# Who sums the routed rows of tiles 4 to 7 before the second attention: DVE in its prologue, or GpSimd ahead of its first affine

## The reference

```
x = x + tanh(g_xattn[0]) * L0_xattn(layernorm(x), ctx)   # 16 heads of 128
x = x + tanh(g_ffn[0])   * L0_ffn(layernorm(x))          # 64 experts, top 8 of them, and a shared MLP
x = x + tanh(g_xattn[1]) * L1_xattn(layernorm(x), ctx)   # 16 heads of 16, 48 + 16 keys
x = x + tanh(g_ffn[1])   * L1_ffn(layernorm(x))          # 8 experts, top 2, and a shared one
```

## Time and profile before

| what | us |
|---|---|
| median of 3 runs (1355.36 to 1357.71) | 1356.01 |
| profiled execution: its span | 1354.8 |
| PE busy | 1046.2 (77%) |
| DVE busy | 765.6 (57%) |
| ACT busy | 424.9 (31%) |
| POOL busy | 307.7 (23%) |

### The profile page before, as it was taken

How to read it: one execution, slowest core, us unless ns; L and a number is a source line. 1 busy time by engine, 2 the same in 40 slices (tenths; PEclk the granted TensorE clock), 3 DMA queues, 4 the chain that set the end, 5 groups by cost and what they waited for, 6 DMA issues and landing times.

```text
span 1354.8 us, 16681 instructions
## 1 busy us (share of the span) xinstructions
PE 1046.2 (77%) x5397; PEld 863.6 (64%) x5397; DVE 765.6 (57%) x1687; ACT 424.9 (31%) x781; POOL 307.7 (23%) x271
## 2 busy tenths in 40 slices
PE   3989989989885700578772377877879999999997
PEld 2867867868663500467661246464757989899896
DVE  6367567585658889323226897786865324242221
ACT  3554445374533300112120032323252232322321
POOL 0413304223000000577771182630200000000000
PEclk8999989999986755788786565768676989899899
DMA  7008600000000140477765640100000000000001
GB/s 264 1 0 288 211 1 0 0 0 1 1 0 20 39 129 1 142 213 223 213 196 185 245 157 32 64 0 0 0 0 1 1 1 0 0 0 0 0 0 62
DMA packets 63667, 91.24 MB, mean 67 GB/s; under 512 B 5901, under 2 KB 56327, under 8 KB 60807
## 3 DMA queue, kind: packets, MB, share of 16 engines
q1 hardware_dynamic: 56116, 71.42, 16.3%
q0 software_dynamic: 6144, 18.88, 4.5%
q10 hardware_dynamic: 1363, 0.37, 0.1%
HBM read 60.74 MB, written 29.89 MB: 67 GB/s over the span
## 4 chain that ended last, share of the span: by engine, by line
PE 55%; DVE 20%; issue 10%; ACT 5%; POOL 4%; DMA 4%; ACTq 1%; DVEq 0%; POOLq 0%; SPq 0%
PE bank L1993 12%; PE bank L2012 7%; PE bank L1651 4%; PE bank L1696 4%; DMA xg<-table,src_now 3%; PE bank L1921 3%; PE bank L1681 2%; PE bank L1879 2%; PE bank L2004 2%; DVE y_sum L1170 2%; PE bank L1798 2%; PE bank L1938 2%; PE bank L1811 2%; POOL q_lo L481 2%; DVE cand L946 1%
## 5 line engine op out<-in xcount | busy, mean ns | idle before, releaser
L1993 PE MATMUL bank<-gu_hi,xnT_split 128*128 128x352 f32 x640 | 159.5, 329 | 0.0
L481 POOL TENSOR_TENSOR q_lo<-soft,q_hi 128x512 fp32r<-128x512 f32 x64 | 93.2, 1456 | 250.2 <-ACT soft L1355 249.9
L1993 PEld LDWEIGHTS bank<-gu_hi,xnT_split 128*128 128x128 f32 x640 | 113.3, 191 | 1.0 <-issue 0.7
L492 POOL DMA_INDIRECT xg<-table,src_now x64 | 62.4, 975 | 222.4 <-DVE src_now L971 203.2
L1233 DVE SCALAR_TENSOR_TENSOR soft<-sg,combine_w,bank 128x176 f32<-128x176 f32 x160 | 56.5, 394 | 88.2 <-PE bank L1993 82.6
L1993 PE MATMUL bank<-gu_lo,xnT_split 128*128 128x352 f32 x320 | 104.2, 325 | 0.0
L2012 PE MATMUL bank<-dn,attnT 128*128 128x256 f32 x448 | 101.2, 384 | 0.0
L751 DVE COPY qT<-bank 128x512 f32<-128x512 f32 x64 | 44.2, 690 | 85.9 <-PE bank L1696 84.8
L2012 PEld LDWEIGHTS bank<-dn,attnT 128*128 128x128 f32 x448 | 85.5, 194 | 11.2
L671 DVE SCALAR_TENSOR_TENSOR x<-bank,gates,x 128x256 f32 (+1 forms) x48 | 22.8, 482 | 114.6 <-PE bank L2012 95.2
L1553 ACT ACTIVATE sg<-bank 128x352 f32<-128x352 f32 x80 | 37.2, 465 | 153.6 <-PE bank L1993 153.6
(11 more groups left out here) (259 smaller groups left out, 2261.6 us busy)
## 6 DMA issues: line engine op xcount, KB each, us to landing
y<-zeros SPq DMA_DIRECT2D x16, 1024.0 KB, 10.8
y_rows<-y SPq DMA_DIRECT2D x16, 1024.0 KB, 4.8
w_gu<-in_L_ffn_w_gu SPq DMA_DIRECT2D x32, 352.0 KB
w_dn<-in_L_ffn_w_down SPq DMA_DIRECT2D x32, 176.0 KB
gu<-in_L_gu SPq DMA_DIRECT2D x1, 3520.0 KB, 12.9
table<-xw SPq DMA_DIRECT2D x4, 640.0 KB
wq<-in_L_xattn_Wq SPq DMA_DIRECT2D x1, 2048.0 KB, 12.6
wo<-in_L_xattn_Wo SPq DMA_DIRECT2D x1, 2048.0 KB, 20.5
```

What stands on the lines that cost most here:

```text
L481: pool.tensor_tensor(q2_lo[:, h % 3, :], q2[h % 2], q2_hi[:, h % 3, :], ALU.subtract).then_inc(q2_split, 1)
L492: pool.indirect_dma_start(xg[:, q, e, :], None, table, bass.IndirectOffsetOnAxis(ap=src_now[:, q, e:e + 1], axis=0)).then_inc(xg_loaded[q] ...
L1993: mm = pe.matmul(b[:, 0:2 * F1], v[:, c, j * P:(j + 1) * P], w[:, c, p, o, :], start=(n == 0), stop=(n == len(terms) - 1))
```

## The change

GpSimd calls `combine(1)`, for tiles 4 to 7, before `affine_queries(0)`, and for that waits until DVE has used tiles 0 to 3. DVE's prologue loses the four calls of `add_up` for tiles 4 to 7; it still waits for `y2_used` to reach 8 ahead of `normed(1)`. The constants that count operations of the chain on either engine are adapted; no other operation changes.

```diff
@@ combine
-                    r, base = y2_rows[:, j % 2], 4 * (G * (i - 2) + j)
+                    r, base = y2_rows[:, j % 2], 4 * (G * (i - 1) + j)
@@ gpsimd
             pool.memset(ctx1T[:], 0.0).then_inc(mask_step, 1)
+            pool.wait_ge(y2_used, G)
+            combine(1)
             affine_queries(0)
             key_blocks(0)
-            pool.wait_ge(y2_used, 2 * G)
             with pool.Fori(1, NG - 1) as i:
@@ vector
             normed(0, EPS0)
-            add_up(G)
             project_queries()
             centre(0)
-            add_up(G + 1)
             deviation(0)
             scale_keys()
             scale_queries()
-            for j in range(G + 2, 2 * G):
-                add_up(j)
             dve.wait_ge(y2_used, 2 * G)
             normed(1, EPS0)
```

More of the change, by code:

```diff
@@ L1156, in attention @@
                 assert last or ch.k == ATT_CHAIN, ch.k
-            ATT_BASE = ROUTE_BASE + ROUTE_CHAIN * NG - NORMED_CHAIN + 1 + 2 * G
+            ATT_BASE = ROUTE_BASE + ROUTE_CHAIN * NG - NORMED_CHAIN + 1 + G
             ATT_CHAIN = FRONT_CHAIN + 5 * G
-            ch.at(ATT_BASE - 1 - 2 * G)
+            ch.at(ATT_BASE - 1 - G)
             for q in range(4):
@@ L1189, in _ @@
             scale_queries()
-            for j in range(G + 2, 2 * G):
-                add_up(j)
             dve.wait_ge(y2_used, 2 * G)
             normed(1, EPS0)
-            assert ch.k == 1 + 2 * G + FRONT_CHAIN + NORMED_CHAIN
+            assert ch.k == 1 + G + FRONT_CHAIN + NORMED_CHAIN
             with dve.Fori(0, NG - 2) as i:
```

## The result

The changed kernel takes 1360.19 us (median of 20 runs, 1357.78 to 1362.79), the kernel before 1356.47 us (median of 20 runs beside them, 1349.74 to 1361.26). The ratio is 1.0032, with a 95% interval of 1.0018 to 1.0046: slower by 4.3 us, between 2.4 and 6.2. Forecast were 1361.0, slower by 5.0.

A forecast was written before the change was run, and what follows sets the result against it. DVE was taken to bound the stretch. PE's L1838 (2.1) and exclusion after 800 (2.9) sum to +5.0 us; span 1354.8 + 5.0 = 1359.8, plus 1.2 for the median, gives 1361.0 us, range 1355 to 1365.5.

The forecast's parts named there:

- The gross gain: DVE without `add_up` of tiles 4 to 7: 0, 2.6 and 9.5 us, at most 12.1 us if nothing takes its place.
- Group 0's layer norm beside GpSimd: `normed(0)` on DVE held up by GpSimd's additions of tile 4: 6.2 us longer, bounds 0 and 7.
- Tile 6's load behind the weights: SP issues it at 755.27 behind the fourth block's weights; it lands at 764.0, so GpSimd idles for 7 us.
- From 764 to the affine: DVE's `deviation` beside GpSimd's tiles 6 and 7 ends at 781.3, 8.6 us late; bounds 4.4 and 11.
- Group 1's layer norm: `normed(1)` on DVE beside both affines, four key blocks and tile 8: 15 us, so `soft2_front(0)` starts 2.2 us later.
- The scores, the exponential, L1838: Group 0's scores start 8.5 us later, the first exponential 6, and L1838 on PE ends 2.1 us late for DVE.
- the limit of 6.4 us: Up to about this lateness of the scores, the route through the first exponential to `soft2_back(0)` costs nothing.
- The exclusion after 800: GpSimd's shifted tiles 8 to 11 hit DVE's softmax of tiles 1 and 2 and the next `centre`: 2.9 us.
- That GpSimd's queue alone decides: Rival: exclusion slight, affine at 777.2 (+4.4); faster by 2 to 4 us, time about 1353; chance 0.10.
- That all tiles flow without a wait: Rival: no wait for tile 6, GpSimd done at 770, affine at 771; about 8 us gained, 1348; chance 0.03.
- That there is no difference: Rival: same chain, but additions meet DVE less after 800 and L1838 runs at high clock: 0 to 2.7 us, 1357.5; chance 0.16.
- A clock at 1.2 GHz throughout the scores: Rival: PE clock stays low through the scores, 3.5 us more there; slower by 8 to 10 us, 1365; chance 0.11.

The follow-up runs named there:

- no_sums: Changed kernel with the sums of tiles 4 to 7 left out on GpSimd, which only waits for each load and counts on; 0.9962 of the kernel before.
- after_wait_xn0: Changed kernel, but GpSimd starts tile 4 only when `xn` of group 0 is written; 1.0015 of the kernel before.
- weights_last: Changed kernel, but SP issues the loads of tiles 6 and 7 ahead of the fourth block's weights; 0.9997 of the kernel before.
- all_pool_spaced: Changed kernel; tile 4 waits for group 0's `xn`, loads of tiles 6 and 7 precede the weights, later groups' sums wait for the layer norm; 0.9990 of before.
- memsets: Changed kernel with GpSimd's operations for tiles 4 to 7 replaced by write-only memsets of the same buffers, sums left out; single run 1360.6 us.
- before_wait_xn: Kernel before, but GpSimd starts a group's sums only when the layer norm of the group before it is written; 0.9990 of the kernel before.

## Why the prediction was right

- **The gross gain.** Put at 12.1 us at most. `no_sums` has DVE 12.2 us earlier at group 1's layer norm, 9.0 at `soft2_front(0)`, and 5.9 at the end of the stretch. The 2.6 us for tile 5 came out as such. What is missing went into DVE operations that GpSimd held up, not into new waits for PE or ACT: DVE's rows have 0.33 us of them ahead of L1084, and 1.21 ahead of `deviation`, as before (1.20).
- **Group 0's layer norm beside GpSimd.** Taken over from group 1's in the trace of before because both have the same alignment: +6.2 forecast, +6.3 measured, and `after_wait_xn0` takes it away. This step carries the prediction: the price stood in the old trace, at another place.
- **Tile 6's load behind the weights.** 7 us of idle time forecast, 7.34 seen. `weights_last` shows it to be worth 4.3 us in the stretch. I had named it as what keeps GpSimd from being done before 777; more exactly, it moves tiles 6 and 7 from DVE's idle time to beside `deviation`.
- **From 764 to the affine.** +8.6 forecast, +8.5 measured; the 3.24 us that GpSimd waited for L1059 confirm that DVE is the later one.
- **Group 1's layer norm.** Put at 15 us beside the affines, the key blocks and tile 8, measured 15.0. `no_sums` has the same 15.0, so this cost comes with DVE's earlier arrival there. In `all_pool_spaced`, where tile 8 waits, the affines and key blocks alone still make it 11.3, against 5.7 undisturbed.
- **The scores, the exponential, L1838.** All within 0.5 us of the forecast. That lateness of the scores costs nothing by itself fits the rows, in which DVE does not wait for ACT or PE there; the limit of 6.4 us was not tested.
- **The exclusion after 800.** The term with the weakest base, 2.9 us: from `soft2_back(0)` to `deviation` of group 1 the shift grew from 1.8 to 4.5, that is by 2.7, of which 2.1 us lie between `soft2_back(0)` and `soft2_front(2)`, where L1087 took 3.90 us at 805.12. L1077 took 4.38 at 811.81, another 1.9 more than before, and 1.4 us of waits for PE's projection (0.30 and 1.06 before) are gone in return. The sum of the forecast put 2.1 us on PE's L1838 as what binds, and there it had the wrong engine: L1835 of the changed kernel ended at 806.84, and PE then waited 2.32 us for DVE's L1087. DVE's own +1.8 stood in its place. That the two differ by no more than 0.3 us is luck.
- **The rivals.** That GpSimd's queue alone decides, with the exclusion slight, fell by `after_wait_xn0` and `memsets`. That all tiles flow without a wait fell by 7.34 us. That there is no difference (0 to 2.7 us) just touches the interval, which begins at 2.4; its mechanism is not in the rows, where the additions held DVE longer after 800, not shorter, and L1835 took 4.54 us, not half of 4.89. A clock at 1.2 GHz throughout the scores did not come: PE took 9.09 us for them, less than the 10.10 of the earlier trace rows.
- **Left open.** Behind the stretch the profiled pair gives 2.2 us of the 4.5 back by the next group's first maximum (117.1 against 119.4 us from the start), in a part where PE ran its matmuls faster in the profile after (the last L1918 of group 0 took 2.20 us for 16 matmuls, the like before 3.62). The medians lie 3.7 us apart and the ratio makes 4.3. Whether such a gift is systematic can't be told from one profile of each.

## What to carry to other kernels

Work that goes from DVE to an idle GpSimd is not free for DVE: look in the trace at what DVE does in the very microseconds in which GpSimd would run, and prefer those in which DVE waits for PE, or does reductions. Put it in front of a GpSimd step on which PE waits only for as long as that engine is idle anyway. Two tiles there, begun once the layer norm was written, won 5 us; four begun in the same way were 2.0 us slower (not clear of noise), and four as in the change 4 us slower. Look as well at what DVE will meet when it gets somewhere earlier: about half of the 12 us that `no_sums` takes from DVE, and over half of the 6.6 us of `before_wait_xn`, went into collisions that had not been there. Before a load is moved onto an engine that will ask for it early, read in which place it stands in its queue.

## What the runs showed of the hardware

I had forecast with one exclusion and found two that differ by the kind of both operations: beside a GpSimd memset of 1.80 us a DVE `tensor_scalar` on 4 numbers per partition took 1.83 us, and a `tensor_tensor` of the same size 0.16. It also goes the other way: GpSimd's multiplication, 0.94 us in most rows, took 2.15 us beside DVE's L1033 of 1.49 us. And an engine's busy time can rise when work is taken from it: DVE 765.6 to 768.0 us with eight instructions fewer.
